# Loading the first batch by chunk, summing squares ahead of the embedding, and giving VectorE the last two steps' convolutions

## The reference

```python
x = x + attention(x, cond)      # RMS norm, scale/shift from cond @ W_emb + b_emb, 16 heads, q/k norms, o + o @ W_out
x = x + gru(cond, x)            # h0 = cond; 512 sequential steps over time
x = x + causal_conv(x, cond)    # depthwise, 4 taps; y[t] = sum_k w[k] * x[t - 3 + k], w = cond
x = x + causal_conv(x, cond) + b3
```

```python
scale, shift = split(emb @ W_emb + b_emb, 2)
xn = x * rsqrt(mean(x * x, -1) + EPS) * g_norm * (1 + scale) + shift
qkv = xn @ W_qkv
```

```python
r = sigmoid(i_r + h_r); z = sigmoid(i_z + h_z)
n = tanh(i_n + r * h_n)
h = (1 - z) * n + z * h
```

## Time and profile before

| | |
|---|---|
| median of three runs | 2163.62 us |
| profiled execution, its own time | 2165.77 us |
| its span, first to last instruction | 2164.0 us |
| TensorE busy | 2091.8 us (97%) |
| VectorE, ScalarE, GpSimd busy | 64%, 54%, 52% |
| mean granted clock of TensorE | 0.994 |

### The profile page before, as it was taken

How to read it: one execution, slowest core, us unless ns; L and a number is a source line. 1 busy time by engine, 2 the same in 40 slices (tenths; PEclk the granted TensorE clock), 3 DMA queues, 4 the chain that set the end, 5 groups by cost and what they waited for, 6 DMA issues and landing times.

```text
span 2164.0 us, 183094 instructions
## 1 busy us (share of the span) xinstructions
PE 2091.8 (97%) x76192; PEld 1575.2 (73%) x76192; DVE 1384.6 (64%) x5127; ACT 1174.7 (54%) x5995; POOL 1128.8 (52%) x3891
## 2 busy tenths in 40 slices
PE   7999999999999999999999999999999999999997
PEld 2222222222389999999999999999999999998886
DVE  3343444444267777777777777777777777777775
ACT  3445445443255555555555555555555555555555
POOL 0143332333146666666666666666666666666665
PEclk9999999999999999999999999999999999999999
DMA  6000000001122222222222121222121212210001
GB/s 253 2 1 1 1 2 1 1 21 60 36 63 52 54 52 52 52 54 51 67 54 57 48 55 49 58 59 65 49 57 49 56 47 62 64 32 6 5 7 19
DMA packets 217582, 95.89 MB, mean 44 GB/s; under 512 B 170120, under 2 KB 213384, under 8 KB 216712
## 3 DMA queue, kind: packets, MB, share of 16 engines
q1 hardware_dynamic: 217272, 92.53, 16.3%
q10 hardware_dynamic: 208, 2.13, 0.3%
HBM read 26.30 MB, written 12.58 MB: 18 GB/s over the span
## 4 chain that ended last, share of the span: by engine, by line
PE 63%; DVE 8%; issue 1%; POOL 0%; DMA 0%; SPq 0%; POOLq 0%; ACT 0%; DVEq 0%
PE ps L1162 57%; DVE arena L1011 5%; PE ps L1190 4%; PE ps L1201 2%; DVE arena L1017 1%; DVE arena L1023 1%; DVE arena L1028 1%; DMA arena<-arena 0%; POOL arena L1234 0%; SPq L939 0%; POOL arena L1238 0%; POOL arena L1240 0%; POOL arena L1244 0%; POOL arena L1247 0%; POOL seq L1250 0%
## 5 line engine op out<-in xcount | busy, mean ns | idle before, releaser
L1162 PE MATMUL ps<-whh,arena 128*4 128x128 f32 (+1 forms) x65536 | 1448.2, 246 | 36.8 <-DVE arena L1028 32.8
L1162 PEld LDWEIGHTS ps<-whh,arena 128*4 128x4 f32 x65536 | 1300.3, 87 | 142.9 <-DVE arena L1028 64.5
L1011 DVE STREAM_TRANSPOSE arena<-ps 128x128 f32<-128x128 f32 x1024 | 436.6, 426 | 226.3 <-PE ps L1162 226.1
L1120 ACT ACTIVATE arena<-arena 128x8 f32<-128x8 f32 x1024 | 215.8, 211 | 637.2 <-DVE arena L1011 637.0
L1234 POOL TENSOR_TENSOR arena<-tap,seq 128x32 f32<-128x32 f32 x1024 | 232.1, 259 | 216.5 <-DVE seq L1041 216.5
L427 DVE TENSOR_REDUCE top<-ps 128x2 f32<-128x1024 f32 x128 | 150.7, 1219 | 253.1 <-PE ps L683 253.1
L1028 DVE TENSOR_TENSOR_SCAN arena<-arena 128x24 f32<-128x24 f32 x1024 | 213.8, 209 | 145.1 <-ACT arena L1131 145.1
L1095 ACT ACTIVATE ps<-arena 128x128 f32<-128x128 f32 x1026 | 269.7, 263 | 0.4 <-PEq L206 0.4
L1234 POOL TENSOR_TENSOR arena<-tap,arena 128x32 f32<-128x32 f32 x1024 | 232.2, 259 | 66.8 <-POOL arena L1244 66.8
L1017 DVE STREAM_TRANSPOSE arena<-ps 128x64 f32<-128x64 f32 x1024 | 257.5, 252 | 12.6 <-PE ps L1162 2.6
L264 POOL TENSOR_TENSOR arena<-arena 128x2048 f32<-128x2048 f32 x16 | 72.8, 4548 | 352.1 <-ACT arena L337 352.1
(11 more groups left out here) (90 smaller groups left out, 1386.8 us busy)
## 6 DMA issues: line engine op xcount, KB each, us to landing
arena<-arena SPq DMA_DIRECT2D x216, 114.0 KB, 2.2
arena<-arena SPq DMA_DIRECT2D x112, 128.0 KB, 2.2
arena<-seq SPq DMA_DIRECT2D x224, 55.0 KB, 2.0
arena<-gi_d SPq DMA_DIRECT2D x248, 32.0 KB
gi_d<-arena SPq DMA_DIRECT2D x96, 57.0 KB
seq<-in_x SPq DMA_DIRECT2D x4, 1024.0 KB, 17.6
out<-seq SPq DMA_DIRECT2D x14, 256.0 KB
whh<-in_w_hh SPq DMA_DIRECT2D x1, 3072.0 KB, 21.6
```

The lines of the kernel that those rows point to most:

```text
L1011: e.transpose(trn[:, h].rearrange("p q (i c s) -> p q c i s", c=2, s=2)[:, :, :, :, 0], bank[RN[h]][:, 0:P].rearrange("p (q c i) -> p q c ...
L1120: e.activation(r_d0[:, h].rearrange("p (i s) -> p i s", s=2)[:, :, 1], trn[:, h, 0, 0:2 * NH].rearrange("p (i s) -> p i s", s=2)[:, :, 0], ...
L1162: last = e.matmul(bank[dst[h]][32 * G:32 * G + B, 0:n], hv, wv[:, k, gates, G, 64 * h:64 * h + 64], start=False, stop=k2 == 1 and k == C - ...
```

## The change

In the prologue: each of the four chunks of batch 0 of `x` gets a load and a semaphore of its own, two issued by SyncE and two by ScalarE. `wemb` comes in four loads, issued by ScalarE behind the two chunks and ahead of the load of its activation table. SyncE's load of `vecT` now comes third, and the weights of the projections are issued once the second chunk of `wemb` has landed. ScalarE's squares wait for one chunk each, TensorE does `sums_x(0)` before the matmuls of the embedding, and these wait for one chunk of `wemb` each.

At the end: the GpSimd loop has 255 turns instead of 256, and VectorE does the convolutions of the last two steps after its loop of steps, with a `tensor_reduce` in place of the two folding additions. The last store waits for VectorE's semaphore `s_end`.

```diff
             @block.sync
             def _(e):
+                for c in range(0, 2):
+                    e.dma_start(seq_cb[:, c, 0, PAD:TP], x[:, c, 0, :]).then_inc(l_x0[c], 16)
                 e.dma_start(vecT[:].rearrange("p c r -> p (c r)"), vec).then_inc(l_vec, 16)
-                e.dma_start(seq_cb[:, :, 0, PAD:TP], x[:, :, 0, :]).then_inc(l_x[0], 16)
+
+                e.wait_ge(l_emb[1], 16)
                 for c in range(2):
...
                     for c in range(C):
+                        if b == 0:
+                            e.wait_ge(l_x0[c], 16)
                         e.activation(xsq[:, c], seq_cb[:, c, b, PAD:TP], ACT.Square).then_inc(a_xsq, 1)
...
+                for c in range(2, C):
+                    e.dma_start(seq_cb[:, c, 0, PAD:TP], x[:, c, 0, :]).then_inc(l_x0[c], 16)
+                for k in range(C):
+                    e.dma_start(wemb[:, k].rearrange("p q G n -> p (q G n)"), w_emb[:, 2 * D * k:2 * D * k + 2 * D]
+                                ).then_inc(l_emb[k], 16)
                 e.preload_act_table_set("natural_log_exp_and_others")
-                e.dma_start(wemb.rearrange("p k q G n -> p (k q G n)"), w_emb).then_inc(l_emb, 16)
                 squares_x(0)
...
+                sums_x(0)
                 e.wait_ge(d_const, 4)
                 e.wait_ge(l_vec, 16)
-                e.wait_ge(l_emb, 16)
                 for k in range(C):
+                    e.wait_ge(l_emb[k], 16)
                     for G in range(NG):
...
                 last.then_inc(p_emb, 1)
-                sums_x(0)
...
+            if first + n < T:
+                e.wait_ge(st["s_pool"], POOL_OPS * ((first + n) // 2))
+            else:
+                e.wait_ge(s_end, END_OPS)
...
+                t, done = T - 2, s_end
+                products = prd[:, 0].rearrange("p (k i s) -> p k i s", k=TAPS, s=2)
+                total = prd[:, 1, 0:2 * NI].rearrange("p (i s) -> p i s", s=2)
+                e.wait_ge(st["s_pool"], POOL_OPS * (T // 2 - 1))
+                e.wait_ge(st["s_x3"], T)
+                n = 0
+                for src in (seq, seq2):
+                    for k in range(TAPS):
+                        e.tensor_tensor(products[:, k], tap[:, k], src[:, :, t + k:t + k + 2], ALU.mult).then_inc(done, 1)
+                    n += TAPS
+                    e.wait_ge(done, n)
+                    e.tensor_reduce(total, prd[:, 0].rearrange("p (k w) -> p w k", k=TAPS), AX.X, ALU.add).then_inc(done, 1)
+                    e.wait_ge(done, n + 1)
...
-                with e.Fori(0, T // 2) as it:
+                with e.Fori(0, T // 2 - 1) as it:
```

More of the change, by code:

```diff
@@ L100, in build @@
         PQ, PK, SS, OB = 4, 5, 6, 7
-        l_vec, l_emb, l_v, l_out = sem("l_vec"), sem("l_emb"), sem("l_v"), sem("l_out")
-        l_x = [sem(f"l_x{b}") for b in range(B)]
+        l_vec, l_v, l_out = sem("l_vec"), sem("l_v"), sem("l_out")
+        l_emb, l_x0 = [[sem(f"{n}{k}") for k in range(C)] for n in ("l_emb", "l_x0_")]
+        l_x = [sem(f"l_x{b}") for b in range(1, B)]
         l_qk = [sem(f"l_qk{c}") for c in range(C)]
@@ L215, in _ @@
                     e.dma_start(wqk[:, c].rearrange("p s k n -> p (s k n)"), w_qk[:, c, :]).then_inc(l_qk[c], 16)
-                e.dma_start(seq_cb[:, :, 1, PAD:TP], x[:, :, 1, :]).then_inc(l_x[1], 16)
+                e.dma_start(seq_cb[:, :, 1, PAD:TP], x[:, :, 1, :]).then_inc(l_x[0], 16)
                 e.dma_start(wout.rearrange("p k n -> p (k n)"), w_out).then_inc(l_out, 16)
                 for b in range(2, B):
-                    e.dma_start(seq_cb[:, :, b, PAD:TP], x[:, :, b, :]).then_inc(l_x[b], 16)
+                    e.dma_start(seq_cb[:, :, b, PAD:TP], x[:, :, b, :]).then_inc(l_x[b - 1], 16)
                 e.dma_start(whh[:].rearrange("p k n -> p (k n)"), w_hh).then_inc(s_whh, 16)
@@ L284, in squares_x @@
                 def squares_x(b):
-                    e.wait_ge(l_x[b], 16)
                     if b:
+                        e.wait_ge(l_x[b - 1], 16)
                         e.wait_ge(p_xs, C * b)
                     for c in range(C):
+                        if b == 0:
+                            e.wait_ge(l_x0[c], 16)
                         e.activation(xsq[:, c], seq_cb[:, c, b, PAD:TP], ACT.Square).then_inc(a_xsq, 1)
@@ L915, in build @@
         n_moving = tile([P, 2, CW])
-        POOL_OPS = 9
-        s_store = sem("out_store")
+        POOL_OPS, END_OPS = 9, 5 + 2 * TAPS
+        s_store, s_end = sem("out_store"), sem("s_end")
         stores = [(P * i, P, 4 * j, 4) for i in range(TB - 1) for j in range(4)]
@@ L924, in store @@
         def store(e, first, n, item, items):
-            e.wait_ge(st["s_pool"], POOL_OPS * ((first + n) // 2))
+            if first + n < T:
+                e.wait_ge(st["s_pool"], POOL_OPS * ((first + n) // 2))
+            else:
+                e.wait_ge(s_end, END_OPS)
             e.dma_start(out[:, item:item + items, first:first + n], seq[:, item:item + items, first:first + n]).then_inc(s_store, 16)
@@ L1084, in _ @@
                         step(it * 2 + v, v)
+                t, done = T - 2, s_end
[11 more added lines that the diff above has]
+                    e.wait_ge(done, n + 1)
+                    if src is seq:
+                        e.tensor_tensor(seq2[:, :, t + PAD:T + PAD], seq[:, :, t + PAD:T + PAD], total, ALU.add).then_inc(done, 1)
+                        n += 2
+                    else:
+                        e.tensor_tensor(total, total, b3x[:], ALU.add).then_inc(done, 1)
+                        e.wait_ge(done, n + 2)
+                        e.tensor_tensor(seq[:, :, t:T], seq2[:, :, t + PAD:T + PAD], total, ALU.add).then_inc(done, 1)
+                        n += 3
+                    e.wait_ge(done, n)
             @block.scalar
```

## The result

The changed kernel's median is 2156.42 us (2154.03 to 2159.75, 7 runs), that of the kernel before 2165.55 us (2162.48 to 2167.61, 7 runs). The ratio is 0.9964, 95% interval [0.9954, 0.9974], or 7.8 us (5.6 to 10.0) less. 6.6 us were forecast. The fastest and the slowest run lie 5.1 us apart in the kernel before and 5.7 us in the changed one.

A forecast was written before the change was run, and what follows sets the result against it. The recurrence, 3.03 us a step, stays unchanged, so only the chain's start and what follows its last step count. Gains of 3.5 + 3.1 = 6.6 us off 2165.77, less 2.15 to the median, give 2157.0 us (2152.8 to 2160.6).

The forecast's parts named there:

- Step 1: Start: the first chunk of x lands at about 5.3 us, the table load hides behind it, TensorE starts at about 6.0.
- Step 2: Start: TensorE's sums run partly at the low clock, take 5.7 us and end at 11.7.
- Step 3: Start: the embedding, at the high clock, ends at 13.5; its last weights must land by 13.0, cover about 1.9 us.
- Step 4: Start: the embedding becomes the late arm; scale_x starts at 14.5 instead of 18.06, 3.5 us gained.
- Step 5: Start: the first projection follows at 16.15; holding back its weights costs nothing, cover 0.6 to 3 us; the clock falls again.
- The end: After the last step: thirteen VectorE operations take 2.5 us, replacing GpSimd's 5.33 and 0.27 us before them; 3.1 us gained.
- the two prices for the multiplications: VectorE's tail: four multiplications take 0.5 us if overlapped, as forecast, or 0.8 us by the skill's drain rule.
- The store behind it: End: the last store begins its packets about 0.8 us after issue, behind earlier stores; its 3.7 us stay.
- the chunks in series: Rival, loads at the start: one queue's chunks pay fixed parts one after another; 2168.1 us, chance 0.05.
- the late clock: Rival, start: sums and embedding all run at 1.2 GHz, so the start gains only 0.6 us; 2159.9 us, chance 0.09.
- the costly tail: Rival, end: VectorE's tail costs about what GpSimd's did, 0.3 us gained there; 2159.8 us, chance 0.06.
- The surviving clock: Rival, first projection: TensorE's clock stays up through the shorter idle time, saving 1.7 us; 2155.3 us, chance 0.18.

The follow-up runs named there:

- e9: The changed kernel itself, measured again on a second chip: median 2155.60 against 2163.22 us for the kernel before, ratio 0.9964.
- e12: The changed kernel itself, measured again on a third chip: median 2155.56 against 2166.04 us for the kernel before, ratio 0.9960.
- e5: The changed kernel with 80 small matmuls of ones on TensorE ahead of the sums; median 2157.78 us, ratio 0.9977 to the kernel before.
- e10: The changed kernel with 52 small matmuls of ones on TensorE ahead of the sums; one run, 2154.67 us.
- e4: The changed kernel with the embedding's matmuls ahead of the sums, loads unchanged; median 2161.22 us, ratio 0.9987 to the kernel before.
- e3: The changed kernel without SyncE's wait for the second chunk of the embedding's weights; median 2161.06 us, ratio 0.9991 to the kernel before.
- e7: The changed kernel with two folding additions in place of each reduction in VectorE's tail; median 2157.36 us, ratio 0.9969 to the kernel before.
- e2: The kernel before with only the end's part of the change; median 2162.27 us, ratio 0.9990 to the kernel before.
- e1: The kernel before with only the prologue's part of the change; median 2160.32 against 2164.05 us, ratio 0.9984.
- e8: The changed kernel with one load each for batch 0 of x and the embedding's weights, other SyncE loads waiting for all those weights; one run, 2162.64 us.
- e11: The changed kernel plus 52 small matmuls, weights held until the embedding's third chunk, last store split into 30 and 2 columns; median 2159.36 us, ratio 0.9975.

## Why the prediction was right

It forecast 2157.0 (2152.8 to 2160.6) and it was 2156.4. That the two lie only 0.6 us apart is partly luck. The forecast started from the three-run median of 2163.62, and the kernel before measured 2165.55 in this comparison; 6.6 us off that would have been 2159.0. The gain by the ratio was larger than forecast, and the two differences have opposite signs. What was right is the mechanism and the size of what the edits do. By its steps:

- Step 1, the first square: landing at 5.3 and TensorE at 6.0. Measured 5.09 and 5.87. The six issues took 3.0 us instead of 2.5, and the table load ended at 5.08, so it, and not the landing, was the later one in this trace; a smaller cover than I saw, without a cost.
- Step 2, the sums: 5.7 us forecast, 6.34 measured, the clock having risen some 5.5 us after the first matmul and not 4.6; 6.20 and 5.34 in e9 and e12. Reading the clock from the pace, against a column that shows 1.00, was right: e5 and e10 show 3.61 us for the same work.
- Step 3, the embedding: end forecast 13.5, measured 13.9, from the sums' delay. The last chunk's landing was forecast by 11.1. In the changed kernel the fourth load landed 8.4 us after its issue at 3.3, so at 11.7; e4 shows it at 11.5, e10 and e5 at 12.2 and 12.6, in the kernels where TensorE waits for it. Against the forecast's 13.0 the cover was 1.3 us (0.4 to 1.5 over these traces) and not 1.9.
- Step 4: scale_x at 14.5 forecast, 15.0 measured; 3.1 us gained, not 3.5. Step 5, no wait for the first projection's weights: right. What I left out of this step is what the wait for the embedding's second chunk buys, 5 us by e3. I costed it as a risk alone.
- The end: 2.5 us forecast, 2.67 measured (each of the two reductions took 0.37 instead of 0.29; leaving the loop, from the end of the addition to the first product, took 0.11 against a forecast of 0.1). Of the two prices for the multiplications, 0.5 and 0.8 us, the trace has 0.51: the early start shown by the small copies holds, and the drain rule of the Trainium skill ("VectorE: DVE Perf Modes", section "The DRAIN you can't avoid"), taken in its first half alone, does not, here.
- The store behind it: 3.6 us against a forecast of 3.7. Its packets begin 1.1 us after the issue (2148.58 to 2149.7), not 0.8; that changes nothing, since the same 1.1 to 1.2 us are in the kernel before. So 6.1 us of edits against 6.6, each term a little too large.

The rivals: the chunks in series didn't come about (a chunk of x landed after 3.9 us, those of the embedding after 7.4 in the median). The clock rose before the sums were done in every trace of this prologue, and VectorE's tail took 2.67 us, so neither the late clock nor the costly tail came about. The surviving clock, at 0.18, is what the profiled execution has: 5.3 us in the first projection. It isn't an alternative to the forecast but something that an execution has or not (e12, e7). My setting it up as one case for the median was wrong in kind; the median lies over both.

What stays open: the gain by the ratio, 7.8 us, is above the edits' 6.1, at an interval from 5.6 on. One possibility is that the prologue changes how often the clock falls in the first projection, which is worth 1.7 us (7.0 against 5.3). With the old idle time of 3.27 us ahead of it (before, e2, e4) it was at 0.50 in all three traces. With 2.7 us it stayed at 1.00 in four (changed, e1, e9, e10) and fell in five (e5, e7, e8, e11, e12). That fits, but three traces against nine don't settle it, and only many traces of both kernels would. The stretch behind the first keep shows no such tie to the prologue: where scale_x came at 18.1 or later (before, e2, e3, e4, e8) it takes 576.0 to 579.1 us, and where it came by 15.2 (all others) 576.0 to 580.1. In the recurrence a step takes 3.03 to 3.04 us on average in each trace; of the 1.0 us there, 0.6 lie in its first three steps, which take 13.1 us before and 12.6 after. Over all fourteen traces that stretch takes 1548.2 to 1551.5 us.

## What to carry to other kernels

Where two chains meet and share an engine, give it first the work whose data can be there first, and order the loads in the same way. Here the order, the chunks and the wait that holds back later transfers were all needed: without one of them 3.4, 5.6 or 5.0 us were lost at scale_x. For a small tail of dependent work on a slow engine, hand it to the one that has just become free. Before claiming a gain of a few microseconds, split it by marks and compare unchanged stretches: here half of the gain in one trace lay in code that nobody had touched.

## What was not expected of the hardware

- Four loads of 512 KB with 4 KB a partition, sharing the DMA engines with other queued loads, lost badly: the last landed at 17.9 beside them (e3) and near 11.5 without (e4), although one load of 2 MB beside the same queue landed at 8.8 in the kernel before. Why is not shown.
- Splitting a store of 32 columns into 30 and 2 made the end 2.5 us later, all of it after the last packet.
- TensorE's low clock after the start lasts differently in one program: the same 32 instructions took 6.34, 6.20 and 5.34 us in three traces of the changed kernel.
